# Two mixture-of-experts layers: gate weights carried behind each token's row, results scaled inside the expert loop and added by accumulating transfers

## What is computed

```python
t = t + _L2_ffn_ref(_ln_t(t), ...)    # mixture of experts "d": 8 experts, best 2, hidden 256
t = t + _L3_attn_ref(_ln_t(t), ...)   # linear attention "e", 8 heads
t = t + _L3_ffn_ref(_ln_t(t), ...)    # mixture of experts "f": 8 experts, best 2, hidden 512
```

```python
logits = flat @ router_w.T
topk_vals, topk_idx = jax.lax.top_k(logits, K)
topk_w = jax.nn.softmax(topk_vals, axis=-1)
y = jnp.einsum('esh,ehd->esd', jax.nn.silu(g) * u, w_down)
out = jnp.einsum('esd,se->sd', y, dense_w)      # dense_w: topk_w at the chosen experts
```

## Time and profile before

| | before |
|---|---|
| median of 3 runs | 969.69 us (969.58 to 978.5) |
| the profiled execution's own time | 975.88 us |
| its span, first to last instruction | 974.1 us |
| mean granted TensorE clock | 0.871 |
| busy PE / DVE / ACT / POOL | 746.4 / 544.4 / 456.9 / 437.2 us |
| "d" experts, POOL's first gather to last result | 390.1 to 550.9 us |
| linear attention, POOL's first gather to DVE's last instruction | 553.6 to 664.9 us |
| "f" route | 670.0 to 725.2 us |
| "f" experts, POOL's first gather to its last scatter | 726.1 to 944.9 us |
| "f" combine, SP's first load to the end of the span | 950.2 to 974.1 us |

### The profile page before, as it was taken

How to read it: one execution, slowest core, us unless ns; L and a number is a source line. 1 busy time by engine, 2 the same in 40 slices (tenths; PEclk the granted TensorE clock), 3 DMA queues, 4 the chain that set the end, 5 groups by cost and what they waited for, 6 DMA issues and landing times. The chain is left out here.

```text
span 974.1 us, 17847 instructions
## 1 busy us (share of the span) xinstructions
PE 746.4 (77%) x4853; PEld 590.5 (61%) x4853; DVE 544.4 (56%) x1589; ACT 456.9 (47%) x1147; POOL 437.2 (45%) x464
## 2 busy tenths in 40 slices
PE   3797978989998736769999535566479999999960
PEld 1575846666665535446666424554367888888850
DVE  6587946777775559354444255776573333333326
ACT  1994435767775314444444334552144444444424
POOL 5000444655652060434444277831015666666734
PEclk9899887999997755899999867987559999999995
DMA  2000000000000240452222211102201111111107
GB/s 97 1 0 19 3 1 2 2 0 0 0 1 2 77 140 1 119 147 64 66 66 66 54 49 50 49 16 76 98 8 34 44 44 47 42 47 41 50 19 259
DMA packets 34197, 46.24 MB, mean 47 GB/s; under 512 B 8227, under 2 KB 22887, under 8 KB 33872
## 3 DMA queue, kind: packets, MB, share of 16 engines
q1 hardware_dynamic: 25264, 27.66, 8.8%
q0 software_dynamic: 8864, 17.72, 6.9%
HBM read 30.21 MB, written 15.60 MB: 47 GB/s over the span
## 5 line engine op out<-in xcount | busy, mean ns | idle before, releaser
L1809 POOL DMA_INDIRECT d_xg<-d_normed,d_gather x71 | 68.3, 961 | 104.5 <-PE ps L1852 79.6
L1047 DVE TENSOR_REDUCE negmax<-ps 128x2 f32<-128x512 f32 x128 | 82.6, 688 | 51.9 <-PE ps L881 51.1
L1809 POOL DMA_INDIRECT f_xg<-f_normed,f_gather x71 | 69.0, 971 | 78.5 <-SPq L1763 55.0
L1908 ACT ACTIVATE f_silu<-ps 128x512 f32<-128x512 f32 x71 | 42.5, 598 | 118.9 <-PE ps L1862 118.9
L1937 DVE TENSOR_TENSOR f_x_low<-ps,f_x_high 128x128 fp32r<-128x128 f32 x71 | 20.7, 292 | 135.5 <-ACT f_x_high L1914 135.5
L1815 POOL DMA_INDIRECT f_results<-f_y,f_scatter x71 | 71.9, 1013 | 54.4 <-issue 39.3
L788 ACT ACTIVATE prob<-ps 128x512 f32<-128x512 f32 x128 | 69.6, 598 | 44.4 <-PE ps L900 44.4
L1261 POOL DMA_INDIRECT e_yg<-d_results,d_slot_u x64 | 61.0, 953 | 32.9 <-issue 18.2
L1883 PE MATMUL ps<-f_w_out,f_hT 128*128 x568 | 75.2, 275 | 0.7 <-DVE f_y L1949 0.7
L1883 PEld LDWEIGHTS ps<-f_w_out,f_hT 128*128 128x128 f32 x568 | 69.0, 192 | 0.9 <-issue 0.9
L1937 DVE TENSOR_TENSOR d_x_low<-ps,d_x_high 128x128 fp32r<-128x128 f32 x71 | 20.6, 290 | 73.6 <-ACT d_x_high L1914 73.6
(11 more groups left out here) (353 smaller groups left out, 2105.0 us busy)
## 6 DMA issues: line engine op xcount, KB each, us to landing
d_results<-d_y SPq DMA_DIRECT2D x71, 64.0 KB
f_raw<-in_f_in SPq DMA_DIRECT2D x16, 256.0 KB, 2.8
f_ys<-f_results SPq DMA_DIRECT2D x8, 512.0 KB, 7.3
X<-in_x SPq DMA_DIRECT2D x4, 512.0 KB, 5.5
d_normed<-X SPq DMA_DIRECT2D x8, 256.0 KB, 2.0
d_raw<-in_d_in SPq DMA_DIRECT2D x8, 256.0 KB, 2.8
f_normed<-X SPq DMA_DIRECT2D x8, 256.0 KB, 2.0
f_w_out<-in_f_out SPq DMA_DIRECT2D x1, 2048.0 KB, 8.2
```

Source lines behind the costliest of these rows:

```text
L1047: nc.vector.tensor_reduce(negmax[:, :, h // HG, col:col + 1], ps[:, 2 + h % 2, :].rearrange("p (t k) -> p t k", t=2), AX_X, ALU.max, negat ...
L1809: nc.gpsimd.indirect_dma_start(xg[:, n % 4, :], None, moe.xn_dram, bass.IndirectOffsetOnAxis(ap=moe.gather[:, n:n + 1], axis=0)).then_inc( ...
L1908: nc.scalar.activation(silu[:, n % 2, :], GATE(n), ACT.Silu).then_inc(silu_ready, 1)
```

## The change

Both layers now write 136 values a token to HBM: the 128 normalised ones and, behind them, the token's eight gate weights (zero for experts not chosen). DVE makes that table (`gates`) in `route`, and SP stores it. Gathered rows bring it along; a small multiply-and-sum with a one-hot row of the tile's expert (`of_tile`) picks each slot's weight in the expert loop (`slot_gates`, on DVE), and the result copy becomes a multiplication by it. A gather waits for `slot_gates` of the tile that had its buffer, besides the transpose.

In "f", `T` is first stored whole to the output (SP, at the start of `route`), and each scatter adds its 128 rows to the output rows of their tokens. Two scatters can now meet in a row, so each waits until the one before it has landed. `combine` is gone, and with it `f_results`.

In "d" the results still go to slot order; in `linear_attention` POOL's four gathers of an image add to `T` as they land. The second pair for an image is issued after the first pair of the next one, and waits until its own first pair has landed. `combine_first` and `e_yg` are gone, and the add of the heads moves from POOL to DVE (`add_tokens`).

```diff
-            def gather(n):
-                if n >= 4:
-                    pool.wait_ge(combined, n - 3)
+            def add_rows(c, n):
+                if c == 1:
+                    pool.wait_ge(added[0][n % 4], 32 * (n // 4 + 1))
...
+                    nc.gpsimd.indirect_dma_start(
+                        T[:, tile, :], None, first.y_dram,
+                        bass.IndirectOffsetOnAxis(ap=first.slot[:, c, tile:tile + 1], axis=0),
+                        compute_op=ALU.add).then_inc(added[c][n % 4], 16)
...
-            for n in range(4, N + 8):
+            for n in range(2, N + 1):
                 if n < N:
-                    gather(n)
-                if n >= 8:
-                    add_output(n - 8)
+                    add_rows(0, n)
+                add_rows(1, n - 1)
...
             def moments(at, first_item, last):
-                dve.wait_ge(combined, at.n + 1)
+                dve.wait_ge(added[1][at.b4], 32 * (at.round + 1))
...
+            def add_tokens(at, first_item, last):
+                dve.wait_ge(heads_ready, at.n + 3)
+                t = T[:, bass.ds(2 * at.n, 2), :]
+                nc.vector.tensor_tensor(t, t, heads[:, at.b], ALU.add).then_inc(tok_ready, 1)
...
+            if out is not None:
+                sp.dma_start(out.rearrange("(t p) c -> p t c", p=P), T[:]).then_inc(tokens_stored, 16)
+            rows_of = moe.xn_dram.rearrange("(t p) c -> p t c", p=P)
...
-                sp.dma_start(groups[g], xn[:, g * GROUP:(g + 1) * GROUP, :]).then_inc(xn_stored, 16)
+                sp.dma_start(rows_of[:, tiles, 0:C], xn[:, tiles, :]).then_inc(xn_stored, 16)
...
+            sp.wait_ge(gates_ready, 1)
+            sp.dma_start(rows_of[:, :, C:], gates[:]).then_inc(gates_stored, 16)
...
+            dve.wait_ge(ratio_ready, 1)
+            step(nc.vector.tensor_scalar(share[:, 0], ratio[:], 1.0, None, ALU.add))
+            step(nc.vector.reciprocal(share[:, 0], share[:, 0]))
+            step(nc.vector.tensor_tensor(share[:, 1], ratio[:], share[:, 0], ALU.mult))
+            step(nc.vector.tensor_tensor(gates[:], chosen[:, 0], by_tile(share[:, 0]), ALU.mult))
+            step(nc.vector.tensor_tensor(same[:], chosen[:, 1], by_tile(share[:, 1]), ALU.mult))
+            nc.vector.tensor_tensor(gates[:], gates[:], same[:], ALU.add).then_inc(gates_ready, 1)
...
+            nc.vector.tensor_scalar(moe.of_tile[:, :, 0:1], passed[:, :, 0:1], -1.0, 1.0, ALU.mult, ALU.add)
+            nc.vector.tensor_tensor(moe.of_tile[:, :, 1:], passed[:, :, 0:E - 1], passed[:, :, 1:], ALU.subtract)
...
             def gather(n):
                 if n >= 4:
                     pool.wait_ge(xT_ps, n - 3)
+                    pool.wait_ge(gate_ready, n - 3)
...
             def scatter(n):
+
                 pool.wait_ge(y_ready, n + 1)
+                if n > 0:
+                    pool.wait_ge(stored[(n - 1) % RING], 16 * ((n - 1) // RING + 1))
                 nc.gpsimd.indirect_dma_start(
-                    moe.y_dram, bass.IndirectOffsetOnAxis(ap=moe.scatter[:, n:n + 1], axis=0),
-                    y[:, n % RING, :], None, bounds_check=TOK * moe.TOP - 1,
-                    oob_is_err=False).then_inc(stored[n % RING], 16)
+                    out, bass.IndirectOffsetOnAxis(ap=moe.scatter[:, n:n + 1], axis=0),
+                    y[:, n % RING, :], None, bounds_check=TOK - 1, oob_is_err=False,
+                    compute_op=ALU.add).then_inc(stored[n % RING], 16)
...
+                nc.vector.tensor_tensor_reduce(product[:], xg[:, n % 4, C:], moe.of_tile[:, n, :], 1.0, 0.0,
+                                               ALU.mult, ALU.add, gate[:, n % 4:n % 4 + 1]).then_inc(gate_ready, 1)
...
-                nc.vector.tensor_copy(y[:, n % RING, :], Y(n)).then_inc(y_ready, 1)
+                dve.wait_ge(gate_ready, n + 1)
+                nc.vector.tensor_scalar(y[:, n % RING, :], Y(n), gate[:, n % 4:n % 4 + 1], None,
+                                        ALU.mult).then_inc(y_ready, 1)
```

More of the change, by code:

```diff
@@ L1135, with __init__ @@
     SLOT_TILES = (TOP * TOK + E * (P - 1)) // P
-    def __init__(self, nc, k, hidden, tag, tables):
+    def __init__(self, nc, k, hidden, tag, tables=None):
         self.F = hidden
@@ L1141, in __init__ @@
         self.w_high, self.w_low = (k.sb(f"{tag}_{s}", [P, self.E, 2 * hidden], F32R) for s in ("w_high", "w_low"))
[L1142 to L1146, removed]
+        self.slot = tables.slot if self.by_slot else None
+        self.xn_dram = nc.dram_tensor(f"{tag}_normed", [TOK, C + self.E], F32, kind="Internal").ap()
+        self.y_dram = (nc.dram_tensor(f"{tag}_results", [P * self.SLOT_TILES, C], F32, kind="Internal").ap()
+                       if self.by_slot else None)
     def allocate_lists(self, k):
@@ L1378, in _ @@
                 dve.sem_inc(s, 1)
-            for s in (sum_ready, heads_ready):
+            for s in (sum_ready, heads_ready, tok_ready):
                 dve.sem_inc(s, 2)
@@ L1446, in statistics, with route @@
                 token_statistics(nc, top, at.n)
-            pipeline(dve, [(-2, shifts), (0, features), (1, sums), (-3, combine_first), (-3, moments),
-                           (2, normalise), (3, statistics)], N, 4)
-def route(nc, top, moe, router_dram, w_out_dram, split=None):
+            pipeline(dve, [(-2, shifts), (0, features), (1, sums), (-3, moments),
+                           (2, normalise), (3, add_tokens), (3, statistics)], N, 4)
+def route(nc, top, moe, router_dram, w_out_dram, split=None, out=None):
     T, ps, ident = top.T, top.ps, top.ident
@@ L1488, in route @@
         ratio = sb("ratio", [P, TILES])
+        share = sb("share", [P, 2, TILES])
+        gates = sb("gates", [P, TILES, E])
         scan = sb("scan", [P, 2, TILES, E])
@@ L1542, in _ @@
                     split.load(sp, i)
+            sp.wait_ge(gates_ready, 1)
+            sp.dma_start(rows_of[:, :, C:], gates[:]).then_inc(gates_stored, 16)
             sp.wait_ge(xn_stored, 16 * (TILES // GROUP))
+            sp.wait_ge(gates_stored, 16)
+            if out is not None:
+                sp.wait_ge(tokens_stored, 16)
         @block.gpsimd
@@ L1746, in _, with experts @@
             nc.vector.tensor_scalar(empty[:], token[:], 0.0, NEVER, ALU.is_equal, ALU.mult)
-            step(nc.vector.tensor_scalar(target[:], token[:], 2.0, -2.0, ALU.mult, ALU.add))
-            step(nc.vector.tensor_tensor(target[:], target[:], empty[:], ALU.add))
-            nc.vector.scalar_tensor_tensor(moe.scatter[:], found[:, 1], 0.0, target[:], ALU.is_gt, ALU.add)
-def experts(nc, top, moe, split=None):
+            step(nc.vector.tensor_scalar(target[:], token[:], 1.0, None, ALU.subtract))
+            nc.vector.tensor_tensor(moe.scatter[:], target[:], empty[:], ALU.add)
+def experts(nc, top, moe, split=None, out=None):
     ps, ident = top.ps, top.ident
@@ L1956, in _ @@
                     hidden(n)
+                if n < TILES_IN:
+                    slot_gates(n)
                 if n >= 2:
@@ L2129, in program @@
             second.allocate_lists(Kit(nc, layer))
-            route(nc, top, second, d["f_router"], d["f_out"])
-            experts(nc, top, second)
-            combine(nc, top, second, out)
+            route(nc, top, second, d["f_router"], d["f_out"], out=out)
+            experts(nc, top, second, out=out)
 def kernel(**inputs):
```

108 lines of the change are left out of this document (24 added, 84 removed).

## The result

| | before | after |
|---|---|---|
| median | 969.63 us (4 runs) | 1069.57 us (1065.4 to 1077.34, 4 runs) |
| the profiled execution, its span | 975.88, 974.1 us | 1067.06, 1065.3 us |
| start of the span to POOL's first "d" gather | 390.1 us | 381.5 us |
| "d" experts, to POOL's first row transfer of linear attention | 163.5 us | 164.7 us |
| linear attention, to the first row of the "f" route | 116.4 us | 139.7 us |

The ratio is 1.102, with an interval of 1.092 to 1.111. The forecast was 998 us. Two stages carry the loss, +75.2 and +23.3 us. In the first row the changed kernel is 8.6 us ahead. Of these, 7.8 lie before the "d" route, in code that is the same in both (the route starts at 328.5 and at 320.7 us): TensorE's granted clock from 300 us to there was 0.66 before, so partly at the lower of its two levels, and 1.00 after.

What follows compares the result with a forecast made beforehand. PE was taken to set the pace in the "f" experts, POOL in linear attention until its last gather. Terms +33.0 - 6.5 + 0.5 + 1 = +28.0 on the median 969.7 gave 998 us, range 950 to 1058.

Steps and rivals of the forecast that it cites:

- The scatters become a chain: "f" loop: each scatter waits for the previous landing, so the period is landing time plus 0.80, 3.75 us against PE's 2.94.
- L = 2.95: "f" loop: landing time of an adding scatter, a plain mean of 2.4 us plus 0.55 for reading HBM first.
- The bounds, 2.3 and 4.9: "f" landing time: at least a plain scatter's 2.3 us, at most a whole gather plus a whole scatter, 4.9.
- the range's L of 3.6: Upper end of the range: landing 3.6 us in "f", with 0.3 more an issue, +89 in all, 1058 us.
- I take 0.80 us: "f" loop: time from the semaphore that lets a scatter go to the scatter's start, 0.80 us.
- I put 0.5 us behind it: End of the kernel: 0.5 us from the last scatter's landing to the end of the span, once `combine` is gone.
- +33.0: "f" experts to the end: net loss of 33.0 us from chained scatters, the gain from `combine` included.
- Between nothing and a doubling (...) I take 0.07: Linear attention: extra POOL issue time of an adding transfer, 0.07 us each, 4.5 us for 64.
- POOL's issue of an accumulate is far from 1 us: A stated sign that the forecast is wrong: POOL's issue time for an adding transfer lies far from 1 us.
- Linear attention, the gain of 11: Linear attention: last moments done at 638.4 instead of 649.5, with adds moved to DVE and weighted adds gone, gaining 11 us.
- Route +0.5, expert loops +1: Gate instructions on DVE cost 0.5 us over both routes; gathers waiting for `slot_gates` cost 1 us over both expert loops.
- Much slower: Rival, 0.08: read and write in full series (landing 4.9 us, +162) or an issue that doubles (+60), 1130 to 1190 us.

Runs made afterwards that it cites:

- run 2: Changed kernel, but each "f" scatter adds to rows of its own, with no wait for another scatter, halves not summed; 980.9 us.
- run 8: Changed kernel, with the scatters' bound set once ahead of the "f" loop and the two waits before each scatter swapped; 1032.6 us, ratio 1.069.
- run 3: Changed kernel, but "f" scatters write instead of adding, to rows of their own, with no wait for another scatter; 972.2 us.
- run 1: Changed kernel, but "f" scatters write instead of adding; the wait for the landing before stays; 1003.5 us.
- Run 4: Changed kernel, but linear attention's transfers write into the tokens instead of adding, order and waits kept; 1033.4 us.
- run 7: Changed kernel, but the scatters' row bound is set in a register once ahead of the "f" loop; 1074.8 us.
- run 6: Kernel before, with only the add of the heads in linear attention moved from POOL to DVE; 950.5 us against 968.9, ratio 0.985.
- run 5: Separate kernel timing eight kinds of row transfer on an otherwise idle core; adding ones of 128 rows: issue 1.54 us, landing 3.3.

## Why the prediction was wrong

- **The scatters become a chain: right.** The wait for the landing binds in 56 of 71 scatters and sets the period; run 2 takes it away and the loss with it.
- **"L = 2.95": mis-sized.** I took the forced read as twice 0.3, from the difference of two plain transfers, and nothing for a longer issue. It was 3.35 on average, 0.40 more. Of the later landing, 0.57 is the longer issue, which the sum had not in L at all, and only 0.46 the packets, less than my 0.55; the two errors partly cancel, and it is luck that L came out so near. The bounds, 2.3 and 4.9, held it, and so did the range's L of 3.6: for "f" that end of the range gives 71 x 3.6 - 176.4 = +79, and +75.2 was measured. The range broke in linear attention, where it gives -11 + 19 = +8 and +23.3 was measured.
- **"I take 0.80 us": mis-sized, and misunderstood.** It was 0.88 here, and not a constant of a semaphore: in the rows that I read it from, the MOVE of the bound stands between wait and transfer, and with nothing between them it is 0.27 (run 8). Together with L, and with some starts that waited for `y`, the period was 4.254 and not 3.75: 70 x 0.504 = 35.3 us of the miss in "f".
- **"I put 0.5 us behind it": wrong.** From the start of the last scatter to the end it is 8.3, not 3.45: 4.8 us. POOL's queue shows a drain of 4.96 us behind its last wait. Before, a drain of 3.65 stood at the same place, and could have been read from the gap between the last landing, at 945.99, and `combine`'s first load; I compared with the end of a stage in which SP issues last. So with plain scatters, too, dropping `combine` is worth 30.2 - 6.65 = 23.6 us (run 3), not 27.4. The drain before, then after (durations in ns):

```profile
L1763 POOLq DRAIN  x1: 3647/3647/3647, 946.4 to 946.4; - x1
```

```profile
L1760 POOLq DRAIN  x1: 4960/4960/4960, 1060.1 to 1060.1; - x1
```

- The first scatter starts 17.1 us behind the first gather, was 15.0: 2.1 us that I had no term for. With TensorE's granted clock there at 0.91 before and 0.85 after, only part of it is the change: runs 1, 3, 4, 7 and 8, at 0.92 to 0.93, have 15.9. With the two above: 35.3 + 4.8 + 2.1 = 42.2, the whole difference between +33.0 and +75.2.
- **"Between nothing and a doubling (...) I take 0.07": the step that failed most for its size.** It was 0.595 an issue, 38 us and not 4.5, in linear attention, and in "f" the same 0.57 lies inside the late landing. The value came from a row of a plain scatter, which says nothing of adding; that the issue has to describe more was in the prediction as a rival and was given 0.08. "POOL's issue of an accumulate is far from 1 us" was named as what would make me wrong.
- **Linear attention, the gain of 11: right, and a term beside it missing.** Run 4 gains 15.0. Of these, 10.2 is what I forecast, DVE at its last row earlier. The other 4.8 is POOL's: before, its drain at the end of the stage lasts until 669.70 and DVE starts the "f" route 5.07 us after its last row; with the adds on DVE POOL has drained long before, and the gap is 0.3. Run 6 gains 12.7 in the same way, 8.0 and 4.8; the seven adds were worth 4.2 there and not 4.6 (the last transfer starts 81.3 us after the first, was 85.5). Net +23.3 in place of -6.5. The route's first DVE row, before and after, with its wait:

```profile
669.99 0.22 DVE L151 TENSOR_TENSOR ln_mean<-ln_stats 128x32 f32<-128x32 f32 x1 [5.07 <-PEq L1204]
```

```profile
685.88 0.22 DVE L151 TENSOR_TENSOR ln_mean<-ln_stats 128x32 f32<-128x32 f32 x1 [0.31 <-PEq L1203]
```

- **Route +0.5, expert loops +1: about right.** The "f" route took 0.1 more at the same granted clock of 0.56. The "d" route took 60.8 against 61.6, but at a clock of 0.61 against 0.56; run 6, the old route at 0.61, took 59.4, so the change cost it some 1.4. The "d" stage took 1.2 more, which lies within the 162.5 to 165.0 that the changed kernel and the six runs with the same "d" stage took. Its gathers now start when `slot_gates` lets them go:

```profile
  DVE d_gate L1950: 84.0, 66
```

- **Rivals.** "Much slower" had the right causes at once, a late landing and a longer issue, with about 0.4 and 0.6 of their sizes. Of the Trainium skill's two rules, the first ("DMA: Bandwidth & Descriptors", Anatomy of one DMA) gives an estimate of 2.15 us for 64 KB; 2.3 was measured for a plain scatter and 3.3 for an adding one. (At 2.15 the period would be 2.15 + 0.80 = 2.95, just PE's 2.94.) The second ("Collectives: The Full Stack", The bandwidth ceiling) blames the second source read; here 0.57 of the 1.0 us of later landing has passed before the first packet leaves, and in run 5 half the bytes save 0.2 of 3.3, so that read can make up less than half of it at this size.

## What to carry over

An adding transfer with a list of rows is not a plain one with an add for free: here it cost POOL 0.6 us more to issue and, that included, a scatter landed 1 us later, so it loses wherever POOL's issue or a wait for the landing sets the pace, and is harmless only beside slack of that size. Where an unmeasured operation enters a loop 60 or 70 times, keep its upper bound in the range until a row of that very operation exists. Split a change that bundles a reorder with a new operation: here 12.7 us of stage time lay in the reorder alone (run 6).

## What the runs showed of the hardware

- An adding row transfer: issue 1.54 to 1.59 us (plain 0.94 to 1.02), landing 3.2 to 3.3 (plain 2.3 to 2.6), on an idle core as in the loop; back to back, with two under way at a time, they land no later than one alone (run 5, linear attention). More than half of the later landing is the longer issue: the first packet leaves 0.57 us behind the issue's end either way. Halving the rows takes 0.12 off the issue and 0.4 off the landing; halving the row length takes nothing off the issue and 0.2 off the landing.
- What stands between the late wait and an indirect transfer on POOL costs about half a microsecond. With the landing wait an instruction of its own it was 0.80 us from landing to start (run 7), with a MOVE of the bound in the loop as well 0.88, with the landing marked on the transfer and no MOVE 0.27 (run 8; 0.26 in run 5). From run 7 to run 8 two swapped lines were worth 43 us of stage time; the swap with the bound still set in the loop was not run.
- Behind the last scatter of "f" POOL's queue drains for 3.65 us where the scatters were plain (before, runs 1, 3 and 6) and for 4.96 where they added (after, runs 2, 4, 7 and 8), and what follows the stage, or the kernel's end, waits for it. These are no constants of the kind of transfer: behind the plain gathers of "d" the drain lasts 7.0 us in both kernels. Why they differ stays open.
